# A transformer layer on one core: attention scores on the whole TensorE array, the feed-forward by pairs of tiles, q/k/v in plain float32, and another order of steps

## What is computed

```python
mod = (_silu(L0_c) @ L0_wmod).reshape(4, 6, 1, -1)        # sa, ca, ga, sb, cb, gb
h = _layernorm(x) * (1 + ca) + sa
x = x + ga * attention(h)
h = _layernorm(x) * (1 + cb) + sb
x = x + gb * ffn(h)
```

## Time and profile before

| | us |
|---|---|
| median of 3 runs | 529.86 (525.7 to 532.13) |
| profiled execution, whole | 535.61 |
| its span | 533.6 |
| TensorE matmuls busy | 474.0 (89%) |
| VectorE busy | 354.6 (66%) |
| ScalarE busy | 267.9 (50%) |
| GpSimd busy | 258.9 (49%) |
| mean granted TensorE clock | 0.913 |

### The profile page before, as it was taken

One profiled execution on the slowest core, in us unless ns is written; L12 is line 12 of the kernel. 1 busy time (PEld: TensorE's weight loads), 2 busy tenths in 40 slices (PEclk: granted clock), 3 DMA queues, 4 the chain that ended last, 5 costly groups with the idle time before them and its releaser, 6 DMA issues. The chain is left out here.

```text
span 533.6 us, 8471 instructions
## 1 busy us (share of the span) xinstructions
PE 474.0 (89%) x2844; PEld 339.5 (64%) x2844; DVE 354.6 (66%) x757; ACT 267.9 (50%) x512; POOL 258.9 (49%) x322
## 2 busy tenths in 40 slices
PE   2757887978989999989999999997799999999995
PEld 0346633455656648768865657886457468897875
DVE  1757867388686765497987744989686349674442
ACT  1243334823673794446367577512576782644240
POOL 4390013658452376276252374365555548963131
PEclk9877668985888999997999999998799999999999
DMA  7710001001000010110010011100200000011011
GB/s 242 236 27 1 0 2 42 1 4 42 22 1 1 4 39 1 41 47 20 1 50 1 4 39 41 46 1 1 72 1 1 2 2 1 1 41 39 1 40 41
DMA packets 18349, 15.99 MB, mean 30 GB/s; under 512 B 6266, under 2 KB 16959, under 8 KB 18307
## 3 DMA queue, kind: packets, MB, share of 16 engines
q1 hardware_dynamic: 18306, 15.45, 9.5%
HBM read 11.10 MB, written 4.22 MB: 29 GB/s over the span
## 5 line engine op out<-in xcount | busy, mean ns | idle before, releaser
L851 ACT ACTIVATE PT<-banks 128x1024 f32<-128x1024 f32 (+3 forms) x96 | 74.6, 811 | 44.2 <-PE banks L680 42.2
L758 PE MATMUL banks<-gTh,guhi 128*128 128x512 f32 x176 | 75.3, 428 | 2.1 <-DVE gTl L1177 1.4
L1098 DVE TENSOR_REDUCE mxp<-banks 128x2 f32<-128x1024 f32 (+3 forms) x56 | 62.5, 1144 | 15.2 <-PE banks L653 9.2
L759 PE MATMUL banks<-gTl,guhi 128*128 128x512 f32 x176 | 70.5, 401 | 0.0
L760 PE MATMUL banks<-gTh,gulo 128*128 128x512 f32 x176 | 70.5, 400 | 0.0
L516 POOL TENSOR_SCALAR_AFFINE_SELECT PT<-PT 128x512 f32<-128x512 f32 x32 | 20.6, 645 | 79.1 <-ACT PT L851 78.8
L1189 DVE TENSOR_TENSOR silfft<-silfft,banks 128x512 f32<-128x512 f32 x40 | 27.3, 686 | 31.7 <-PE banks L760 16.9
L653 PE MATMUL banks<-QKT 48*128 48x512 f32 (+3 forms) x192 | 42.5, 478 | 6.5 <-DVE mxp L1098 2.0
L564 PE MATMUL banks<-wdhi,ffhi 128*128 128x256 f32 x160 | 46.7, 292 | 0.7 <-POOL fflo L552 0.7
L680 PE MATMUL banks<-QKT 50*128 50x512 f32 (+3 forms) x192 | 40.8, 447 | 6.9 <-ACT PT L851 2.6
L680 PEld LDWEIGHTS banks<-QKT 50*128 50x128 f32 x192 | 18.9, 198 | 41.9 <-issue 35.4
(11 more groups left out here) (160 smaller groups left out, 1176.9 us busy)
## 6 DMA issues: line engine op xcount, KB each, us to landing
xbuf<-in_L_attn_x SPq DMA_DIRECT2D x8, 512.0 KB, 3.6
out_x<-x SPq DMA_DIRECT2D x8, 512.0 KB, 3.0
wm_st<-in_L_wmod SPq DMA_DIRECT2D x1, 1536.0 KB, 7.3
modB<-mod_scratch SPq DMA_DIRECT2D x4, 256.0 KB, 3.3
wg_st<-in_L_ffn_w_gate SPq DMA_DIRECT2D x1, 704.0 KB, 5.2
wu_st<-in_L_ffn_w_up SPq DMA_DIRECT2D x1, 704.0 KB, 6.3
x<-in_L_ffn_w_down SPq DMA_DIRECT2D x1, 640.0 KB, 4.8
gate_b<-mod_scratch SPq DMA_DIRECT2D x4, 128.0 KB, 3.2
```

Of the source, the lines that this page charges most:

```text
L758: pe.matmul(o[:], guhi[:, k, blk, :], gTh[:, k, cols], start=(k == 0), stop=False)
L759: pe.matmul(o[:], guhi[:, k, blk, :], gTl[:, k, cols], start=False, stop=False)
L851: act.activation(PT[:, u % 2, 2 * q:2 * q + 2, 0:CH - q0], both("prob", b, n)[:, :, 0:CH - q0], ACT.Exp, scale=float(D) ** -0.5).then_inc( ...
L1098: dve.tensor_reduce(dst, both("max", b, n)[:, :, 0:len(at) * kn].rearrange("p e (m k) -> p e m k", k=kn), AX.X, ALU.max).then_inc(S["mxr"], 1)
```

## The change

- **Scores.** `QKT` has now 6 blocks instead of 4: two of queries as before, and four of keys, one for each head, in which the other head's 64 rows are zero. `max` and `prob` read all 128 rows, so a head's matmul uses the whole array and the two of a pair follow one another. VectorE zeroes the unused halves once, at the start. `stack` does two tiles at a time into two banks, and `stk` is three copies of 512 elements for a pair of tiles instead of one for a tile.
- **Feed-forward.** `gate` and `up` work on a pair of tiles: a group is two blocks of 128 feed-forward columns by 256 tokens, 12 matmuls of 256 columns (the last `up` group 6), and needs only its own pair's `h2lo`. `gTh`, `gTl`, `ffhi` and `fflo` hold two pairs, in turn. The elementwise steps work on 512 elements for the first two groups and on two stretches of 256 for the third.
- **q/k/v.** `xT` is copied once (`xev`), `Wq_b` is one plain float32 array, `xlo` and the low weights are gone, and a pair takes 4 float32 matmuls, each of which is two records in a trace, instead of 12 float32r ones.
- **Order.** `ORDER` is another list. Among others `ldA` comes ahead of `ldW`, `ldG` and `ldB` for the first sample, four `norm1` of the first chunk come ahead of GpSimd's `gprep`, and three of ScalarE's `aprep` ahead of its first `xev`.

```diff
-LO_V, LO_P = [0, 2, 4, 5], [1, 3]
-
-
-PE_STEPS = dict(bias=1, xT=NJ, qkv=NJ, stack=NT, max=NM, mtT=NC, prob=2 * NP, pv=NP, yT=NC, ynT=NC, wo=NJ, hT=NJ,
-                a=NT, h2T=NJ, gate=NC * NF, up=NC * FB, down=NT)
-ACT_STEPS = dict(xhi=NJ, sthi=NC, stk=NT, mrow=NC, exp=2 * NP, ycopy=NC, ynev=NC, ms1=NJ, hhi=NJ, ms2=NT, h2=NT, h2hi=NJ,
-                 sil=NC * NF, ffhi=NC * NF)
-DVE_STEPS = dict(wts=1, wob=1, biasq=1, stats=NC, xlo=NJ, qkvb=NJ, rope=NC, stlo=NC, mxr=NM, mneg=NC, ytm=NC, x1=NJ,
-                 norm2=NJ, hlo=NJ, route=NT, hsel=NT, h2lo=NJ, fft=NC * NF, fflo=NC * len(LO_V), sum=NT)
-POOL_STEPS = dict(rstd1=NC, norm1=NT, pmask=ND, rstd2=NJ, hmod=NJ, rs1=NJ, had=NJ, zad=NJ, rs2=NJ, ffl=NC * len(LO_P), fin=NJ)
+NG = 3
+PAIR_T = 2 * P
+
+
+
+GROUPS = [(0, 1), (2, 3), (4, 5)]
+LO_P = 1
+
+
...
-        Wqhi = sb("Wqhi", [P, KB, QKV], F32R)
-        Wqlo = sb("Wqlo", [P, KB, QKV], F32R)
+        Wq_b = sb("Wq_b", [P, KB, QKV])
...
-        xTh = sb("xTh", [P, 2, KB, P], F32R)
-        xTl = sb("xTl", [P, 2, KB, P], F32R)
+        xTc = sb("xTc", [P, 2, KB, P])
...
-        rt = stk[:, :, 0:H, :].rearrange("p t h d -> p t (h d)").rearrange(
-            "p t (m h i) -> p m t h i", m=4, h=2 * H)
-
-        QKT = sb("QKT", [P, 4, T], F32R)
+        rt = stk[:, :, :, 0:4 * HALF].rearrange("p t h (m i) -> p m t h i", m=4)
+
+
+        QKT = sb("QKT", [P, 2 + H, T], F32R)
...
-        gTh = sb("gTh", [P, KB, T], F32R)
-        gTl = sb("gTl", [P, KB, T], F32R)
+        gTh = sb("gTh", [P, 2, KB, PAIR_T], F32R)
+        gTl = sb("gTl", [P, 2, KB, PAIR_T], F32R)
+        sil = sb("sil", [P, 2, CH])
+        fft = sb("fft", [P, 2, CH])
...
-        ffhi = sb("ffhi", [P, NF, CH], F32R)
-        fflo = sb("fflo", [P, FB, CH], F32R)
+        ffhi = sb("ffhi", [P, 2, NF, PAIR_T], F32R)
+        fflo = sb("fflo", [P, 2, FB, PAIR_T], F32R)
...
-                    wait("xlo", n + 1)
+                    wait("xev", n + 1)
                     free(kind, n)
                     o = of(kind, b, n)
                     for t in range(2):
                         for k in range(KB):
-                            i = three_pass(o[:, t * QKV:(t + 1) * QKV], xTh[:, t, k, :], xTl[:, t, k, :],
-                                           Wqhi[:, k, :], Wqlo[:, k, :], t == 0 and k == 0, t == 1 and k == KB - 1)
+                            i = pe.matmul(o[:, t * QKV:(t + 1) * QKV], xTc[:, t, k, :], Wq_b[:, k, :],
+                                          start=(t == 0 and k == 0), stop=(t == 1 and k == KB - 1))
                     i.then_inc(S["qkv"], 1)
                 elif kind == "stack":
-                    if n % TPC == 0:
-                        wait("sthi", n // TPC + 1)
-                        wait("stlo", n // TPC + 1)
-                    free(kind, n)
-                    o = of(kind, b, n)
-                    for q in range(4):
-                        i = pe.transpose(o[:, q * P:(q + 1) * P], stk[:, n % TPC, 2 * q:2 * q + 2, :].rearrange(
-                            "p h d -> p (h d)"), ident[:])
+                    wait("sthi", 2 * n // TPC + 1)
+                    wait("stlo", 2 * n // TPC + 1)
+                    free(kind, n)
+                    o = both(kind, b, n)
+                    for t in range(2):
+                        for q in range(4):
+                            i = pe.transpose(o[:, t, q * P:(q + 1) * P], stk[:, (2 * n + t) % TPC, 2 * q:2 * q + 2, :
+                                             ].rearrange("p h d -> p (h d)"), ident[:])
                     i.then_inc(S["stack"], 1)
                 elif kind == "max":
                     qt, k0, kn, at = MAX_UNITS[n]
-                    wait("stk", qt + 1)
+                    wait("stk", qt // 2 + 1)
                     free(kind, n)
                     o = both(kind, b, n)
                     diag = k0 + kn == (qt + 1) * P
                     for m, q in enumerate(at):
                         for e in range(2):
-                            rows = slice(e * HR, e * HR + QK)
-                            i = pe.matmul(o[:, e, m * kn:(m + 1) * kn], QKT[rows, q, qt * P:(qt + 1) * P],
-                                          QKT[rows, 2 + q, k0:k0 + kn], start=(m == 0),
+                            i = pe.matmul(o[:, e, m * kn:(m + 1) * kn], QKT[:, q, qt * P:(qt + 1) * P],
+                                          QKT[:, 2 + 2 * q + e, k0:k0 + kn], start=(m == 0),
...
-                    wait("stk", j + 1)
+                    wait("stk", j // 2 + 1)
                     free(kind, n)
                     o = both(kind, b, n)
                     for e in range(2):
-                        rows = slice(e * HR, e * HR + QKM)
-                        i = pe.matmul(o[:, e, 0:CH - q0], QKT[rows, 2 + q, j * P:(j + 1) * P],
-                                      QKT[rows, q, c * CH + q0:(c + 1) * CH], start=True, stop=True)
+                        i = pe.matmul(o[:, e, 0:CH - q0], QKT[:, 2 + 2 * q + e, j * P:(j + 1) * P],
+                                      QKT[:, q, c * CH + q0:(c + 1) * CH], start=True, stop=True)
...
-                    c, f = (n // NF, n % NF) if kind == "gate" else (n // FB, n % FB)
-                    wait("h2lo", (c + 1) * NJ // NC)
+                    j, g = n // NG, n % NG
+                    wait("h2lo", j + 1)
                     if b == 0 and n == 0:
                         pe.wait_ge(s_setG, weights_split)
                     free(kind, n)
                     o = of(kind, b, n)
-                    cols = slice(c * CH, (c + 1) * CH)
-                    blk = FB + f if kind == "up" else f if f < FB else 2 * FB
-                    for k in range(KB):
-                        pe.matmul(o[:], guhi[:, k, blk, :], gTh[:, k, cols], start=(k == 0), stop=False)
-                        pe.matmul(o[:], guhi[:, k, blk, :], gTl[:, k, cols], start=False, stop=False)
-                        i = pe.matmul(o[:], gulo[:, k, blk, :], gTh[:, k, cols], start=False, stop=(k == KB - 1))
+
+                    blocks = [f if kind == "gate" else FB + f for f in GROUPS[g] if f < FB]
+                    if kind == "gate" and g == NG - 1:
+                        blocks.append(2 * FB)
+                    for m, blk in enumerate(blocks):
+                        for k in range(KB):
+                            out_ = o[:, m * PAIR_T:(m + 1) * PAIR_T]
+                            gh, gl = gTh[:, j % 2, k, :], gTl[:, j % 2, k, :]
+                            pe.matmul(out_, guhi[:, k, blk, :], gh, start=(m == 0 and k == 0), stop=False)
+                            pe.matmul(out_, guhi[:, k, blk, :], gl, start=False, stop=False)
+                            i = pe.matmul(out_, gulo[:, k, blk, :], gh, start=False,
+                                          stop=(m == len(blocks) - 1 and k == KB - 1))
                     i.then_inc(S[kind], 1)
...
-                    c, t = n // TPC, n % TPC
-                    wait("fflo", c * len(LO_V) + len(LO_V) - 2)
-                    wait("ffl", (c + 1) * len(LO_P))
+                    j, t = n // 2, n % 2
+                    wait("fflo", j * (NG - 1) + 1)
                     free(kind, n)
                     o = of(kind, b, n)[:, 0:C]
-                    cols = slice(t * P, (t + 1) * P)
+                    hi, lo = ffhi[:, j % 2, :, t * P:(t + 1) * P], fflo[:, j % 2, :, t * P:(t + 1) * P]
                     for f in range(FB):
-                        if f == FB - 1:
-                            wait("fflo", c * len(LO_V) + len(LO_V) - 1)
-                        three_pass(o, ffhi[:, f, cols], fflo[:, f, cols], wdhi[:, f, :], wdlo[:, f, :], f == 0, False)
-                    wait("fflo", (c + 1) * len(LO_V))
-                    pe.matmul(o, ffhi[:, FB, cols], wdhi[:, FB, :], start=False, stop=False)
-                    pe.matmul(o, ffhi[:, FB, cols], wdlo[:, FB, :], start=False, stop=True).then_inc(S["down"], 1)
+                        if f == GROUPS[LO_P][0]:
+                            wait("ffl", j + 1)
+                        elif f == GROUPS[NG - 1][0]:
+                            wait("fflo", j * (NG - 1) + 2)
+                        three_pass(o, hi[:, f, :], lo[:, f, :], wdhi[:, f, :], wdlo[:, f, :], f == 0, False)
+                    pe.matmul(o, hi[:, FB, :], wdhi[:, FB, :], start=False, stop=False)
+                    pe.matmul(o, hi[:, FB, :], wdlo[:, FB, :], start=False, stop=True).then_inc(S["down"], 1)
...
-                    act.activation(QKT[:, :, n * P:(n + 1) * P], of("stack", b, n).rearrange("p (q n) -> p q n", q=4),
-                                   ACT.Copy).then_inc(S["stk"], 1)
+                    o = both("stack", b, n).rearrange("p t (q n) -> p q t n", q=4)
+                    cols = slice(n * PAIR_T, (n + 1) * PAIR_T)
+                    for rows, to, q in ((slice(0, P), slice(0, 2), 0), (slice(0, HR), slice(2, 2 + H, 2), 2),
+                                        (slice(HR, P), slice(3, 2 + H, 2), 2)):
```

(23 more changed lines are left out.)

246 lines of the change are left out of this document (130 added, 116 removed).

## The result

| | before | after |
|---|---|---|
| median | 531.0 us (4 runs, 525.7 to 532.78) | 511.23 us (4 runs, 509.38 to 514.46) |
| profiled execution, its span | 535.61, 533.6 | 510.83, 509.1 |
| mean granted TensorE clock | 0.913 | 0.970 |

The ratio is 0.965, 95% interval 0.956 to 0.974: faster. Measured once more, it was 0.963 (0.954 to 0.972). The ratios leave out executions over 1.5% above the fastest of the same kernel: 9 of the kernel before's 17 beside `before_plain_keep_xlo`, `by_runs_all_samples` and `after_again`, one of 1391 us of `before_plain_keep_xlo`, and one of `after_first_whole`.

The account below looks back on a forecast made before the run. It took TensorE's queue as the bound, much of it at the low clock. 535.6 - 4 (scores) + 4 (feed-forward) + 0 (q/k/v) - 4 (start) - 21 (clock) = 510.6, less 5.7 to the median: 505 us, range 483 to 535.

Parts of the forecast that it names:

- clock as planned: Whole kernel: the forecast case, all terms as summed, 505 us, own range 492 to 519; chance 0.46.
- the profiled execution is 5.7 above the median, so 505: Last step of the sum: from 510.6 for the profiled execution to 505 us, as the runs' median was 529.9.
- Clock, -21 predicted: Low-clock stretches, mostly 35 to 166 us: whole scores 14, feed-forward pairs 5, small stretches 2; bounds 0 and -41.
- the four stretches of the earlier trace: 33.8 us at low clock with TensorE busy; at 2.4 GHz 17 us would return, 14 were taken.
- the clock doesn't move: Rival: low stretches at 35 to 166 us come from waits and transposes, not half-used rows; 526 us, chance 0.22.
- Scores' own work, -4 predicted: max and prob matmuls: 91.5 us split against 87.4 whole, changes of shape included; worst bound +35.
- 281 changes of shape at 0.20 us, 84 left: Places in ORDER where neighbouring TensorE steps use the array in another shape, 0.20 us each; the 84 are around pv.
- Feed-forward by pairs, +4 predicted: Feed-forward: 528 matmuls of 512 columns become 1056 of 256, +4 us; columns ready after two tiles instead of four.
- q/k/v, 0 on TensorE: q/k/v: eight plain float32 records, 2.56 us, against twelve float32r matmuls, 2.67 us, a pair of tiles; 0 us.
- Start, -4: Before the first qkv matmul: low weights gone 1.96 us, ldA earlier about 1.3, one xlo 0.69; bounds -2 and -6.
- Copies and order, 0: ScalarE's stk copies, +9.5 us, hidden in its idle time; the order taken at 0, bounds -10 and +10.
- The signs that were named: PEclk well above 0.75 at 35 to 166 us, scores 0.23 us apart, gate at 0.12, first qkv near 30 us.

Follow-up runs that it names:

- before_plain_keep_xlo: Kernel before with plain float32 q/k/v matmuls, but xlo and the low weights still made and waited for: 532.51 us, ratio 1.0041.
- by_runs_all_samples: Kernel after with score pairs split, in all samples, only where a count at 0.20 us a change of shape made it cheaper: 506.09 us, ratio 0.9577.
- after_again: Kernel after, unchanged, timed once more for a comparison on one chip: 510.26 us, ratio 0.9634.
- after_first_whole: Kernel after with whole scores for the first sample alone, split pairs of 64 rows for the other three: 510.99 us, ratio 0.9614.
- before_whole_scores: Kernel before with max and prob reading all 128 rows, QKT not enlarged, so two heads are mixed: 522.58 us, ratio 0.9831.
- before_64_rows: Kernel before with 64 instead of 48 and 50 rows in each half of a score pair: 526.81 us, ratio 0.9898.
- after_split_scores: Kernel after with max and prob reading 48 and 50 rows again, pairs in two halves of the array: 513.62 us, ratio 0.9646.
- before_whole_plain: Kernel before with whole scores (two heads mixed) and plain float32 q/k/v without xlo: 517.46 us, ratio 0.9737.
- before_ldA_first: Kernel before with the first sample's ldA ahead of ldW, ldG and ldB on the queue: 533.89 us in one execution, beside a median of 534.16.

## Why the prediction was right, point by point

It said 505 us, 25 below the median it knew; measured were 511.2, 20 below. The likeliest case came, "clock as planned". For the profiled execution the sum was 535.6 - 25 = 510.6, and 510.83 was measured. That is partly luck: two terms were mis-sized in opposite directions, about 11 us each. The 6 us that were missed are the last step, "the profiled execution is 5.7 above the median, so 505". That execution was long because its clock was low (0.913, where others had up to 0.945), and this is what the change took away: the kernel after has no such excess, 510.83 against a median of 511.23. So most likely the same microseconds were subtracted twice.

- **Clock, -21 predicted, -31.8 measured.** The reading of the earlier trace rows was right in kind: stretches in which TensorE is busy throughout and still at 1.2 GHz have to do with how much of the array its matmuls use. before_whole_scores shows it alone (-29.3), before_64_rows shows it with nothing changed but rows. The size was low: if the four stretches of the earlier trace rows gave all of their 17 us, the stretch of 117 to 137 us and the 28.7 us of small ones gave 14 or 15, where I had counted 7. But whole scores, which had 14 of the 21 us in the sum, are not the only way. Without them the other parts already take the price down by 21.9 us (78.1 to 34.4 in after_split_scores), where I had given feed-forward by pairs 5 and the order 0. So the reading of the rival "the clock doesn't move", that the low stretches come from the waits of the old order, was right for part of them.
- **Scores' own work, -4 predicted, +7.6 measured in the new order and +12.7 in the old.** The step that failed is "281 changes of shape at 0.20 us, 84 left". 0.20 came from one kind of place, a pair between feed-forward matmuls, and there it holds (0.62 against 0.46). But I gave the same to all 197. At masks the scores cost nearly the same whole or split (0.88 and 0.94), in a row the split pairs are cheaper (0.85 and 0.93), and on average a vanished change was worth 0.12 us in the old order and 0.14 in the new. By the twofold speed of the Trainium skill, "TensorEngine Tiling (Array Packing)", section "Theoretical Speedup", the loss would have been the 35 us of added columns; the runs show 12.7 and 7.6 of it, since part is saved at changes of shape. The same page, "Key Properties", says that these drain the engine, and gives no price.
- **Feed-forward by pairs, +4 predicted.** `gate` and `up` have 130.3 us of work before and 134.7 in after_split_scores, where the scores around them are split as before: +4.4 (steps from start to start, added up by line, those at 1.2 GHz halved).
- **q/k/v, 0 on TensorE.** Right: 421.4 and 421.5 in before and before_plain_keep_xlo. Four column passes against three, as by "FP8 and Floating Point Precision" of the Trainium skill, section "TensorE Precision Notes", don't show at 192 columns here either.
- **Start, -4.** Right in sum (34.1 to 30.2), not in its parts: `ldA` gave more than its 1.3 us and the weights less. The timeline after:

```profile
24.48 0.88 SPq L407 DMA_DIRECT2D modc<-mod_scratch  x2
27.11 1.15 DVE L1032 TENSOR_SCALAR Wq_b<-Wqkv,modc 128x192 f32<-128x192 f32 x2 [2.38 <-DMA modc<-mod_scratch]
30.23 1.54 PE L631 MATMUL banks<-Wq_b,xTc 128*128 128x192 f32 x8 [1.26 <-ACT xTc L823]
...
34.96 1.25 DVE L1096 TENSOR_TENSOR stk<-qk,cos_t 128x256 f32<-128x256 f32 x1
```

  The weights are ready at 28.26, but now the copy `xTc` is last and ends the wait: I had written that the copy is not what is waited for. Plain q/k/v alone gained 1.1 us (32.9), `ldA` alone 2.9. The first `rope` comes at 34.96 instead of 41.34.
- **Copies and order, 0.** For idle time this holds; the clock that pairs and order gave is told above. ScalarE's `stk` copies are 48 of 590 ns, and TensorE's idle time stays at 39.7 us. In the stage of 108 to 166 us VectorE is busy for 55.28 of 58.0 us, though: this cover is nearly used up.
- **The signs that were named.** PEclk is well over 0.75 between 35 and 166 us and 0.97 on the whole, the first q/k/v matmul is at 30.2, `gate` matmuls go at 0.12, score matmuls at 0.23 (0.46 a pair). All four held, and the term of the scores was wrong all the same: I had named no sign at masks or in rows of pairs.

**What stays open:** which of pairs and order lifts the clock behind 108 us; what it is behind a bf16 mask that costs 0.1 us; and how much of the clock each kind of matmul (`pv`, transposes) would hold by itself.

## What to carry to other kernels

Where TensorE is busy for nearly all of a stretch and the granted clock is still low, count the rows that its matmuls use before counting its waits: work that fills the array with zeros may run slower by itself and end sooner. Other changes can take away the same low clock without adding columns, as the feed-forward by pairs and the new order did here, and then the filling adds nothing: try both with and without it. Once the clock is up, the same filling is a pure cost, so use it only where nothing else holds the clock. The price of changing the array's shape has to be read at each kind of neighbour (feed-forward, mask, another pair), not at the cleanest one and multiplied. And if the profiled execution is longer than the median, ask whether the change removes the reason for that before scaling a forecast by the difference.

## What the runs showed of the hardware

- At equal duration and equal order, pairs of 64 rows leave 57.5 us of busy time at 1.2 GHz where pairs of 48 or 50 rows leave 78.1 (mean clocks 0.940 and 0.922). Whole-array scores, which stream twice the columns, leave 19.5 (0.965). "TensorE: Matmul & The Clock Gate" of the Trainium skill, section "What's actually happening", has the clock follow how busy the engine has been; that agrees with the stretch after 106.9 us, but the busy share by itself doesn't explain these three: from 35.5 to 108 us it is 62.2, 61.5 and 61.2 of 72.5 us, at a clock of 0.75, 0.82 and 0.95.
- In the kernel after, the stretch of 216.1 to 219.5 us is at 1.2 GHz with TensorE busy for 3.40 of 3.40 us, and it holds feed-forward matmuls of 128 rows and `wo`. Just before, TensorE had idled for 3.78 us, as the timeline after shows:

```profile
214.87 0.65 PE L706 MATMUL banks<-ident,ytm 128*65 128x128 f32 x4 [3.78 <-DVE ytm L1138]
```

  So the clock of a stretch isn't told by what runs in the stretch itself.
- Zero rows count: what before_64_rows adds to each half, rows 50 to 63, is zero in the keys, and the clock rises. Half of the rows that whole scores read of the keys are zero in the kernel after, and the clock holds as well as in before_whole_plain, where they are not (14.5 and 11.4 us).
- A plain float32 matmul of 192 columns costs about the same as three of float32r (work of the whole kernels 421.5 and 421.4 us).
- Two VectorE instructions of 128x192 elements took 1.93 us in one place of the order and 0.54 in another, with the same operands (L1010, and the timeline of before_ldA_first); they ran 1.5 us earlier there, and not straight behind the wait for `modc`. In both, GpSimd was making `gulo` (L491). Before, its two products took 1.83 us, from 30.07, and the slow pair lasted as long as they did; in before_ldA_first they took 2.56 us, from 28.39, and the pair on VectorE was through in 0.54. The two engines thus seem to hold each other up, now one and now the other; no run tried it.
